# Order of the reduction matmuls and of one copy in a pipelined state-space scan

## The reference

```python
x = silu(conv(x) + conv_b)                     # x, z = split(h @ in_proj_w.T)
x_dbl = x @ x_proj_w.T                         # dt (128), Bm (16), Cm (16)
dt = softplus(x_dbl[..., :128] @ dt_proj_w.T + 2 * dt_proj_b)
deltaA = exp(dt[..., None] * A)                # A = -exp(A_log)
deltaB_u = dt[..., None] * Bm[:, :, None, :] * x[..., None]
states = scan(s = deltaA * s + deltaB_u)       # along the tokens
y = sum(states * Cm[:, :, None, :], axis=-1) + x * D
out = (y * z) @ out_proj_w.T
```

## Time and profile before

| | us |
|---|---|
| three runs | 2794.95, 2801.03, 2806.85 (median 2801.03) |
| the profiled execution | 2794.95 |
| its span, first to last instruction | 2793.2 |
| TensorE busy | 2512.8 (90%) |
| VectorE busy | 1856.1 (66%) |
| GpSimd busy | 1384.0 (50%) |
| ScalarE busy | 1258.0 (45%) |
| the scan stage in the span | about 1377 to 2355 |

### The profile page before, as it was taken

The page is one execution under the profiler, slowest core; times in us unless marked ns, Lnnn a source line. Parts: engine busy times, 40 slices in busy tenths (PEclk is TensorE's granted clock), DMA queues, the critical chain, the costliest instruction groups (busy, mean ns, idle before and its releaser), DMA issues.

```text
span 2793.2 us, 33262 instructions
## 1 busy us (share of the span) xinstructions
PE 2512.8 (90%) x11786; PEld 1467.7 (53%) x11786; DVE 1856.1 (66%) x2240; ACT 1258.0 (45%) x1997; POOL 1384.0 (50%) x741
## 2 busy tenths in 40 slices
PE   5999939999989999989678899989989888999998
PEld 2455624444677888855233333333433333677776
DVE  4678875554555666665579789889978888722223
ACT  3443205531223666434456655764665452334333
POOL 0222338860040000241299999999999996122221
PEclk9999759998989999999889899999999999999999
DMA  6443683432053777641275676587587565100000
GB/s 223 140 121 102 87 112 88 95 94 105 12 216 128 256 261 259 208 125 51 84 186 160 173 210 182 162 202 217 170 204 213 174 194 191 46 1 16 15 1 31
DMA packets 278967, 384.98 MB, mean 138 GB/s; under 512 B 127104, under 2 KB 148608, under 8 KB 271392
## 3 DMA queue, kind: packets, MB, share of 16 engines
q1 hardware_dynamic: 268944, 335.77, 41.4%
q0 software_dynamic: 9296, 38.80, 5.7%
q10 hardware_dynamic: 576, 8.39, 0.7%
HBM read 312.91 MB, written 59.51 MB: 133 GB/s over the span
## 4 chain that ended last, share of the span: by engine, by line
PE 55%; POOL 15%; DVE 11%; issue 6%; SPq 5%; DMA 4%; ACT 4%; another core or an unknown queue 0%; PEldq 0%; ACTq 0%; DVEq 0%; POOLq 0%; PEld 0%
POOL arena L786 8%; PE psum L2036 8%; POOL arena L792 5%; PE psum L1983 4%; PE psum L2217 4%; PE psum L2218 4%; PE psum L2832 4%; SPq L2293 4%; PE psum L3019 2%; PE psum L2190 2%; PE psum L2191 2%; PE psum L483 2%; PE psum L2823 1%; PE psum L1879 1%; PE psum L2082 1%
## 5 line engine op out<-in xcount | busy, mean ns | idle before, releaser
L786 POOL TENSOR_TENSOR arena<-arena 128x1024 f32<-128x1024 f32 x256 | 626.3, 2466 | 130.9 <-DVE arena L1551 82.7
L2036 PE MATMUL psum<-arena,cst 128*128 128x512 f32 x1024 | 507.4, 631 | 101.4 <-POOL arena L792 90.4
L1090 ACT ACTIVATE psum<-arena,negA 128x512 f32<-128x512 f32 x512 | 333.4, 682 | 319.0 <-DVE arena L1566 276.4
L2036 PEld LDWEIGHTS psum<-arena,cst 128*128 128x128 f32 x1024 | 189.3, 197 | 400.7 <-issue 215.2
L1566 DVE TENSOR_TENSOR_SCAN arena<-psum,arena 128x512 f32<-128x512 f32 x256 | 310.6, 1213 | 58.8 <-ACT psum L1090 37.6
L1566 DVE TENSOR_TENSOR_SCAN psum<-psum,arena 128x512 f32<-128x512 f32 x256 | 298.7, 1212 | 57.8 <-POOL arena L786 55.0
L792 POOL TENSOR_TENSOR arena<-arena 128x1024 f32<-128x1024 f32 x128 | 312.7, 2443 | 3.0 <-DVE arena L1566 3.0
L840 POOL TENSOR_TENSOR arena<-arena 128x512 f32<-128x512 f32 x64 | 92.3, 1442 | 324.2 <-ACT arena L1214 299.2
L1983 PE MATMUL psum<-arena 128*128 128x512 f32 x512 | 231.8, 596 | 1.3 <-PE psum L1983 0.8
L2381 POOL TENSOR_TENSOR arena<-arena,cst 128x512 f32<-128x512 f32 x64 | 76.3, 1216 | 270.2 <-DVE arena L2685 178.9
L2369 POOL TENSOR_TENSOR arena<-arena,cst 128x1024 f32<-128x1024 f32 x96 | 184.8, 1953 | 43.2 <-PE psum L2933 25.9
(11 more groups left out here) (373 smaller groups left out, 5000.7 us busy)
## 6 DMA issues: line engine op xcount, KB each, us to landing
arena<-bc_scr SPq DMA_DIRECT2D x256, 512.0 KB, 5.4
arena<-w_exp SPq DMA_DIRECT2D x23, 1408.0 KB, 6.1
arena<-in_gu SPq DMA_DIRECT2D x48, 512.0 KB, 4.6
arena<-in_inw SPq DMA_DIRECT2D x32, 512.0 KB, 4.4
arena<-in_dn SPq DMA_DIRECT2D x31, 512.0 KB, 6.9
x_scr<-arena SPq DMA_DIRECT2D x19, 512.0 KB, 5.9
arena<-in_x SPq DMA_DIRECT2D x8, 1024.0 KB, 11.6
w_exp<-in_gu SPq DMA_DIRECT2D x16, 512.0 KB, 7.1
```

The lines of the kernel that those rows point to most:

```text
L786: nc.gpsimd.tensor_tensor(dB[:, k % 4], du[:, j:j + 2], BC[:, k % RING, 0].unsqueeze(1).broadcast_to([P, 2, T]), ALU.mult).then_inc(s["db_ ...
L1090: nc.scalar.activation(psum[:, bank], dt[:, b % 2, j + t], ACT.Exp, scale=negA2[:, at:at + 1]).then_inc(s["da_ok"], 1)
L2036: ins = mm(psum[:, t], ident, dB[:, k % 4, t], start=False, stop=(n == NS - 1), skip_group_check=True)
```

## The change

Two things move, and nothing is added or taken away. On TensorE, `sums(b, 2 * p + 1)` comes directly after `sums(b, 2 * p)` at every position, ahead of the position's other matmuls; before, this was so at positions 7, 15, 23 and 31 only. On ScalarE, `bc_out(nx)` at position 23 comes at the head of the list of that position's tasks for the next batch, ahead of `log_next(nx, 0)` instead of behind it.

```diff
--- before.py
+++ after.py
@@ -1158,6 +1158,8 @@
                             first_tap(nx, x_at.index(p - 1))
                         if p == 19:
                             xdt_out(nx)
+                        if p == 23:
+                            bc_out(nx)
                         if p in (20, 21):
                             dt_parts(nx, 2 * (p - 20))
                         if p == 21:
@@ -1167,7 +1169,6 @@
                             minus_linear(nx, 0)
                         if p == 23:
                             log_next(nx, 0)
-                            bc_out(nx)
                         if p in (27, 28):
                             dt_in(nx, 4 + 2 * (p - 27))
                         if p == 28:
@@ -2129,8 +2130,7 @@
                 x_at = X_AT if b else X_FIRST
                 for p in range(UN // 2):
                     sums(b, 2 * p)
-                    if p % 8 == 7:
-                        sums(b, 2 * p + 1)
+                    sums(b, 2 * p + 1)
                     if b and p < 4:
                         z_tile(b - 1, p + 4)
                     if nx and b:
@@ -2169,8 +2169,6 @@
                             dt_tiles(nx, 2 * (19, 20, 26, 27).index(p))
                         if p >= 28:
                             z_tile(b, p - 28)
-                    if p % 8 != 7:
-                        sums(b, 2 * p + 1)
             for m in range(KT):
                 output_last(m)
```

## The result

The change makes the kernel slower by 0.57%: 2818.37 us (median of 18 runs) against 2802.41 for the kernel before on the same chips, ratio 1.0057, 95% interval 1.0044 to 1.0070. That is 16 us more where 8 less were forecast, and it lies past the end of the range (2814). The profiled execution took 2808.16 us, its span 2806.4. The granted clock is no part of it: 0.951 in the mean, 0.950 before.

A forecast was written before the change was run, and what follows sets the result against it. In the scan stage GpSimd, TensorE and VectorE are close to their limit; VectorE paces the convolution stretches. -11.9 - 1.5 + 0 + 5.6 = -7.8 us: 2787 from 2794.95 profiled, 2793 against the median 2801.03; range 2775 to 2814.

The forecast's parts named there:

- (a): Scan stage: odd sums directly behind even ones free GpSimd's odd buffer earlier; -11.9 us at GpSimd's pace, -1.5 in convolution stretches.
- rival 2: TensorE's new wait starves ScalarE's first taps, so VectorE stands in the convolution stretches: +21 us, 2822; chance 0.18.
- (b): TensorE's work behind the odd sums waits for VectorE's product by C, some 60 waits; 0 to 27 us, taken as 0.
- even waits past 27 us: Sign in the new profile: GpSimd's waits for even sums above 27 us would mean (b) was sized too small.
- the far end, 27: Upper bound of (b): each new TensorE wait uses up GpSimd's room at the even buffer, 27 us.
- the 4 that were to be the sign against it: Convolution stretch: VectorE idle for over 4 us would mean that it does not decide there.
- (c): Positions 20 to 24: ScalarE, its queue full, gets the moved work's results 1.72 us later; 1.25 us passes on.
- (d): Position 23: ScalarE stands 3.1 us ahead of the copy, decays 4.5 late; +5.6 us, bounds 0 and 13.5.
- Rival 4: TensorE's clock drops to 1.2 GHz after some 7 of the longest new waits: +12 us, 2805; chance 0.04.
- Rival 1: GpSimd gains nearly all in the scan stage, ScalarE's wait hidden: -17 to -28 us, 2773 to 2784; chance 0.22.
- Rival 3: ScalarE's wait at position 23 costs its far end, 13.5 us, so no change shows, 2801; chance 0.08.

The follow-up runs named there:

- e1: The kernel before with the copy of B and C alone moved ahead of the logarithm at position 23; 2796.31 us, ratio 1.0005.
- e3: The change with the old order of the sums at positions 0 to 3 of each batch; 2803.02 us, ratio 1.0029.
- e13: The kernel before with the new order of the sums at position 0 of batches 1 to 3; timed once, 2801.10 us.
- e15: The kernel before with the new order of the sums at positions 0 and 1 of batches 1 to 3; 2806.39 us, ratio 1.0034.
- e16: The change with GpSimd's three transfers of the second dt half one position later in batches 1 to 3; 2808.85 us, ratio 1.0032.
- e4: The change with SyncE's unit 5 weight load behind the broadcast rows of unit 10 in batches 1 to 3; 2810.15 us, ratio 1.0028.
- e11: The kernel before, new order at positions 18-27 (batch 0), 23-27 (1, 2), 13-31 (3), unit 5's load behind unit 11's rows; 2793.53 us, ratio 0.9970.
- e7: The kernel before with SyncE's unit 5 weight load held until VectorE's scan of unit 5, already done, in batches 1 to 3; timed once, 2803.41 us.
- e9: The kernel before with SyncE's unit 5 weight load held until a later scan, of unit 6, in batches 1 to 3; timed once, 2806.27 us.
- e5: The kernel before with SyncE's unit 5 weight load held until unit 4's product in batches 1 to 3; 2796.69 us, ratio 1.0013.
- e6: The change with the old order of the sums at positions 6 to 17 and 29 of each batch; 2819.3 us, ratio 1.0052.
- e12: The change with the old order at positions 0 to 3, 6 to 17 and 29, and the copy behind the logarithm; 2798.16 us, ratio 0.9985.
- e10: The change with SyncE's unit 5 weight load held until VectorE's product of unit 4 in batches 1 to 3; 2821.78 us, ratio 1.0057.
- e2: The change with the copy back in its old place, so TensorE's new order alone; 2802.87 us, ratio 1.0036.

## Why the prediction was wrong

**The step that is missing: SyncE's path and the DMA engines.** The change part by part goes through TensorE, ScalarE, VectorE and GpSimd and has no term for what a moved instruction does to the transfers. GpSimd 0.45 us earlier at position 1 (wanted, and part of (a)) puts its own megabyte nearer to SyncE's rows, and 19 us of busy DMA engines turn this into 3 to 4.5 us for rows that had 0.15 us of room in batch 2 of the old kernel (0.9 to 2.3 in the three batches of e1). Measured +10.2 in the steps at positions 4 and 5 (e3 takes it away, e13 and e15 bring 6.7 and 9.0 of it back), forecast 0. It is more than half of the loss, and no rival held it; rival 2 had the sign, by another mechanism.

The Trainium skill, "DMA: Bandwidth & Descriptors", section "Issuing engines are not separate DMA queues", says that transfers issued by ScalarE, SyncE or GpSimd run on the same 16 DMA engines and interleave. By e16 this holds here: the same rows take 6.0 to 6.4 us without GpSimd's transfers in flight and 13.1 to 14.5 with them. Its section "Queues, rings and completion order" says that each DMA engine takes the descriptors of SyncE's ring in order; e4 and e11 agree: rows of unit 10 ahead of the load take 7.9 us, and rows of unit 11 take 10.7 ahead of it and 14.3 behind it.

**(a), the odd sums' gain: -11.9 - 1.5.** The waits went as said, 27.9 us to 0. The step that failed is that 11.9 us of them were counted at full value. The even waits grew by 26, nearly as much: in batches 1 and 2 the odd ones were 15.2 us and the even ones 2.5, and now the even ones are 20.2. A position's matmuls and both units' sums take TensorE as long in either order, so the odd buffer comes early, GpSimd goes ahead, and then stands for the even one. That reading is argued; the sums are measured. Measured gains are 10.6 us at most. Of these, 1.6 at position 19 of batch 0 are also in e7 and e9, with the old order, and so are none; of the 5.6 in batch 3, kernels that have the old order there show up to 2.6 as well (e13; 1.4 in e1 and e5), and e16, which has the new one, shows 0.7. What gain there is lies where TensorE has other work than in batches 1 and 2: batch 0 and batch 3 from position 19 on. In batches 1 and 2, where the forecast had a good part of its 11.9, the gains are 0.5 each at positions 0 to 3 and 0.5 each at 24.

**(b), TensorE's wait for VectorE's product: 0.** Mis-sized. 82 waits as against 16, so the count (some 60 more) was right. The prediction's own sign for this came true, even waits past 27 us: they are 44.8, though much of that growth is the odd waits moved over, as under (a). It measured +7.7 us at most. In the convolution stretches the waits cost 3.4 us at most (e3), an eighth of the far end, 27. So the reason given for zero, that VectorE decides there, nearly held, and VectorE's 3.5 us of idle time in the earlier trace rows's stretch stayed under the 4 that were to be the sign against it. Where it broke was one place, 29 to 31, with VectorE's 3.25 us multiply ahead of its product: 4.3 us (e6). That multiply was to be seen in the trace of before, and was not looked for.

**(c), ScalarE later at 20 to 22: 1.25.** Right in kind: +0.8 at position 22 and +0.9 at 19, in batches 1 and 2 each (the 0.8 at 22 stays in e12). The steps between give 0.7 of it back, and 0.5 more at 24 where the copy is in its old place, so that (c) alone is worth about 1 us in all. The sum had it only as a part of (d).

**(d), the copy: +5.6.** The mechanism was right: 3.63 us of wait (forecast 3.1), VectorE's wait 5.73 (over 4), GpSimd standing in batches 0 to 2. The size was 7.1, 1.5 too small, for ScalarE was later still than (c) made it: the decays began 5.5 us later (1818.44 against 1811.97, less the 1.0 by which the traces stand apart at the product of position 21), where the sum had 4.5. e1 shows the other half, that without the new order it costs nothing.

**Rival 4, the clock**: no part of it (0.951 against 0.950). **Rival 1** was wrong for the reason under (a). **Rival 3**: the copy cost half of its far end, 7.1 of 13.5.

With the measured sizes, -10.6 + 10.2 + 7.1 + 5.2 + 4.3 = +16.2; the 1.4 us to the 17.6 of the table are ScalarE's in (c) and small steps. The terms are steps of one execution each, so the tenths are not to be leaned on.

## What to carry to other kernels

A wait on an engine that isn't alone in setting the pace is not a gain to be cashed: ask which buffer that engine wants next, and whether the order behind it makes that one earlier too. Before moving anything, list the transfers whose landing is only just in time (issue and landing against use, not the list of waits) and look at the DMA share in stretches of a few microseconds; half a microsecond on an engine that issues transfers cost ten here. When a static order is changed at every position, try it by position: the same order was worth up to 10 us less in some places and 27 more in others (7 of them with the copy), and a selection of positions with a later load (e11) beat both kernels.

## What the runs showed of the hardware that was not expected

- A transfer of 512 KB from SyncE took 6.0, 7.5, 9.8, 12.7 or 14.5 us, the same instruction each time, by what was in flight around it. The step from 7 to 13 us came with shifts of half a microsecond or less between queues.
- Identical stretches of instructions differ between executions by single jumps of 1.2 to 2.1 us, always at the same few places (in kernels with the old order, against the profile of before: position 8 of batch 0 1.3 us shorter, 17 or 19 of it 1.7 longer or 1.6 shorter, 28 of it 1.2 longer, 8 of batch 3 2.1 shorter; in e13, with the old order in batch 3 from position 1 on, 6, 10 and 17 of it 1.2 to 1.6 longer and 30 of it 1.7 shorter). They make the spread of 960.9 to 965.5 us in the stage of kernels with the old order of the sums.
- Which transfer loses shows in the traffic by queue. The packets of lines 803 and 810 come in two bursts, in the change at 12 to 20 and 23 to 30 us behind the batch's first product. The changed kernel, batch 2, 24 to 28 us, inside the second:

```profile
...
q0 software_dynamic: 90, 0.74, 88.3%
q1 hardware_dynamic: 78, 0.15, 11.2%
...
```

Both queues send about as many packets, but one of GpSimd's (q0) carries four times the bytes and holds an engine seven times as long (an estimate from these lines: 0.63 against 0.09 us). Where a trace has the landing, the rows of unit 10 landed by 25.6 us or at 26.9 and later, never between: before the second burst has taken over, or close to its end. In e16 the same happened to the rows of unit 12, issued at 22 us and landed at 34.4 to 34.9, with GpSimd's packets from about 21.5 to 35. What decides on which side of the burst they fall is not settled: e5 and e10 have load and rows at the same distances within about 0.1 us, and e2's batches 1 and 2, with one order of instructions, landed on different sides (23.8 and 28.0 us).
